# Narrow masked score pairs of the attention's row maxima share two PSUM banks

## The reference

```python
x = L0_attn_x                                   # (8, 1024, 256)
h = _layernorm(x) * (1 + ca) + sa
# attention, per head (16 heads, 48 channels for q and k, 16 for v)
scores = jnp.einsum('bhqd,bhkd->bhqk', q, k) * scale
scores = jnp.where(causal[None, None], scores, -jnp.inf)
attn = jax.nn.softmax(scores, axis=-1)
out = jnp.einsum('bhqk,bhkd->bhqd', attn, v)
x = x + ga * (out @ W_o)
h = _layernorm(x) * (1 + cb) + sb
# experts: t = (h @ Wm + bm) in parts of 32; softmax of logits over 16 experts, two are kept
hmid = gelu(einsum('td,edi->tei', t, W1) + b1); eo = einsum('tei,eio->teo', hmid, W2) + b2
x = x + gb * (comb @ Wo + bo)
```

## Time and profile before

| what | value |
|---|---|
| median of 3 runs | 2950.63 us (2949.89 to 2953.15) |
| span of the profiled execution | 2947.5 us; the page gives no other time for it |
| TensorE busy (modelled ends) | 2823.2 us, 96% |
| VectorE busy | 1869.7 us, 63% |
| ScalarE busy | 1806.7 us, 61% |
| GpSimd busy | 1243.5 us, 42% |
| score pairs of the maxima, L418 | 1536 matmuls |

### The profile page before, as it was taken

The page is one execution under the profiler, slowest core; times in us unless marked ns, Lnnn a source line. Parts: engine busy times, 40 slices in busy tenths (PEclk is TensorE's granted clock), DMA queues, the critical chain, the costliest instruction groups (busy, mean ns, idle before and its releaser), DMA issues.

```text
span 2947.5 us, 51530 instructions
## 1 busy us (share of the span) xinstructions
PE 2823.2 (96%) x16460; PEld 1254.0 (43%) x16460; DVE 1869.7 (63%) x4636; ACT 1806.7 (61%) x2148; POOL 1243.5 (42%) x1325
## 2 busy tenths in 40 slices
PE   6789999999999999999999999999999999999999
PEld 2344444444444444444434444444444444444433
DVE  5665766756667566666666666675756657666553
ACT  1346675566755667456674576655766566655687
POOL 4311555126551364413644146531465225661254
PEclk9889999999999999999999999999999999999999
DMA  6303443034430444204432044321553124531243
GB/s 141 73 1 84 113 121 96 4 98 112 133 73 2 106 123 118 70 8 119 121 100 70 21 128 122 90 56 29 134 130 91 34 63 115 130 84 27 74 129 93
DMA packets 177556, 253.06 MB, mean 86 GB/s; under 512 B 51085, under 2 KB 83869, under 8 KB 177197
## 3 DMA queue, kind: packets, MB, share of 16 engines
q1 hardware_dynamic: 170300, 247.79, 32.9%
q10 hardware_dynamic: 6996, 1.99, 0.3%
HBM read 159.13 MB, written 12.63 MB: 58 GB/s over the span
## 4 chain that ended last, share of the span: by engine, by line
PE 85%; DVE 6%; issue 3%; ACT 2%; POOL 1%; SPq 0%; DMA 0%; ACTq 0%; DVEq 0%; POOLq 0%
PE ps L1236 17%; PE ps L1272 17%; PE ps L1290 16%; PE ps L1256 9%; PE ps L418 8%; PE ps L464 4%; PE ps L505 2%; PE ps L466 2%; PE ps L535 2%; DVE front L561 1%; PE ps L516 1%; DVE rest L1392 1%; PE ps L492 1%; PE ps L523 1%; PE ps L450 1%
## 5 line engine op out<-in xcount | busy, mean ns | idle before, releaser
L1356 ACT ACTIVATE rest<-ps 128x1024 f32<-128x1024 f32 x1024 | 993.7, 1024 | 341.2 <-PE ps L1272 341.1
L1338 ACT ACTIVATE rest<-ps 128x1024 f32<-128x1024 f32 (+3 forms) x768 | 608.6, 810 | 550.1 <-PE ps L1236 536.4
L1456 POOL TENSOR_TENSOR rest<-rest 128x512 f32<-128x512 f32 x478 | 631.9, 1322 | 560.6 <-DVE rest L1392 550.1
L1392 DVE SCALAR_TENSOR_TENSOR rest<-ps,b2c,wide 128x512 f32<-128x512 f32 x512 | 383.8, 750 | 490.4 <-PE ps L1290 460.7
L1272 PE MATMUL ps<-wide,w1s 98*128 98x512 f32 x2048 | 644.6, 434 | 11.5 <-ACT rest L1356 8.7
L1290 PE MATMUL ps<-rest,w2s 128*32 128x512 f32 x4096 | 546.1, 605 | 0.6 <-ACT rest L1356 0.6
L1446 POOL TENSOR_SCALAR_AFFINE_SELECT rest<-rest 128x256 f32<-128x256 f32 x512 | 204.3, 407 | 806.7 <-ACT rest L1338 803.6
L558 DVE CUSTOM_DVE_ANT_0 rest<-ps,maskd 128x256 f32<-128x256 f32 (+3 forms) x1024 | 458.7, 487 | 121.9 <-PE ps L418 114.6
L1236 PE MATMUL ps<-wide 49*128 49x512 f32 (+3 forms) x2304 | 485.7, 511 | 7.2 <-ACT rest L1338 6.1
L1272 PEld LDWEIGHTS ps<-wide,w1s 98*128 98x128 f32 x2048 | 346.0, 189 | 238.4 <-ACT rest L1356 109.4
L561 DVE TENSOR_REDUCE front<-ps 128x1 f32<-128x512 f32 x512 | 329.1, 685 | 103.7 <-PE ps L418 99.9
(11 more groups left out here) (138 smaller groups left out, 2225.0 us busy)
## 6 DMA issues: line engine op xcount, KB each, us to landing
wide<-gate_rows SPq DMA_DIRECT2D x1024, 128.0 KB, 2.8
wide<-front SPq DMA_DIRECT2D x480, 64.0 KB, 2.0
wide<-front SPq DMA_DIRECT2D x192, 128.0 KB, 2.4
ao<-in_x SPq DMA_DIRECT2D x16, 512.0 KB, 5.0
heads<-front SPq DMA_DIRECT2D x64, 128.0 KB, 2.4
xs<-in_x SPq DMA_DIRECT2D x16, 512.0 KB, 5.1
out<-xs SPq DMA_DIRECT2D x32, 256.0 KB, 2.7
wide<-ao SPq DMA_DIRECT2D x96, 64.0 KB, 2.3
```

Source lines behind the costliest of these rows:

```text
L1338: nc.scalar.activation(L.pt[:, u % PTS, :, f:HALF], L.ps[:, 2 * (u % 2):2 * (u % 2) + 2, 0:HALF - f], ACT.Exp, scale=SCALE).then_inc(S["c_ ...
L1356: nc.scalar.activation(L.hm[:, u % HM, :], bank(2 * (u % 2), 2), ACT.Gelu).then_inc(S["e_gelu"], 1)
L1392: v.scalar_tensor_tensor(out=dst, in0=bank(L2 + q % 2), scalar=L.b2c[:, e:e + 1], in1=L.gb[:, q // 2 % GB, q % 2, :], op0=ALU.add, op1=ALU ...
L1456: g.tensor_tensor(dst, dst, L.gy[:, k % GY, :], ALU.add).then_inc(S["e_add"], 1)
```

## The change

The narrow masked pairs are joined two by two. Of the eight masked pairs of a half, the 128-key and the 384-key pair of the same `pr` share their two banks, and so do the two 256-key pairs; the two of 512 keys stay single. An item now carries a tuple of parts, `("pair", g, parts)`. TensorE waits for the two banks once, writes both parts into each bank side by side, four matmuls in direct sequence (first part upper and lower rows, second part upper and lower), and tells VectorE only at the last couple. VectorE reads first bank's parts, then the second bank's, with the same operations as before, and releases a bank after its last part; the wait for the scratch tile's last use stands at the first part alone.

A group has 18 issues for 24: `PAIRS[0]` is 5 items for 8, `PAIRS[1]` 13 for 16, in a new order in which the joined and the masked ones alternate with plain ones. `EARLY` is 3 for 4, so the opening computes a third item with 128 and 384 keys. The places are new: in images 1 to 7 slots 1, 2, 3, 5 and 7 have one item each, between; from slot 9 to 36 every slot has one between, and every even slot a second one behind: 47 items for 62. In the experts 25 of the slots 28 to 62 have an item, for 34.

```diff
--- before.py
+++ after.py
@@ -329,7 +329,18 @@
 
 
 SWAP = [(i + RD // 2) % RD for i in range(RD)]
-PAIRS = [[(i, n, pr) for i in range(4 * c, 4 * c + 4) for n in range(c + 1) for pr in range(2)] for c in range(2)]
+
+
+def masked_pairs(c):
+
+    i = 4 * c
+    shared = [(((i, c, pr), (i + 2, c, pr)),) for pr in range(2)] + [(((i + 1, c, 0), (i + 1, c, 1)),)]
+    return shared + [(((i + 3, c, pr),),) for pr in range(2)]
+
+
+PAIRS = [masked_pairs(0), [(((i, 0, pr),),) for i in range(4, 8) for pr in range(2)]]
+for k, pair in enumerate(masked_pairs(1)):
+    PAIRS[1].insert(2 + 2 * k, pair)
 ROWS = [(0, 0), (0, 1), (1, 0), (2, 0), (3, 0), (1, 1), (2, 1), (3, 1)]
 
 
@@ -369,7 +380,7 @@
                 done[e] += 1
                 self.frees.append((read[e], done[e]))
             self.end[item] = (read[e], done[e])
-            if item[0] == "pair" and item[3] == item[2] // 4:
+            if item[0] == "pair" and item[2][0][1] == item[2][0][0] // 4:
                 self.last_masked[item], masked = masked, item
 
     def last(self, bank):
@@ -408,15 +419,21 @@
     if kind in USES and not USES[kind]:
         return
     if kind == "pair":
-        g, i, n, pr = item[1:]
-        keys = key_range(i, n)
+        g, parts = item[1:]
         for name, count in R.moved[g]:
             pe.wait_ge(S[name], count)
         outs = [ring_write(pe, L, R, item, hh) for hh in range(2)]
-        for hh in range(2):
-            rows = slice(HP * hh, HP * hh + QD)
-            pe.matmul(outs[hh][:, 0:keys.stop - keys.start], L.q2[g][rows, pr, i * P:(i + 1) * P].bitcast(F32R),
-                      L.k2[g][rows, pr, keys].bitcast(F32R), start=True, stop=True).then_inc(S[R.filled], 1)
+        at = 0
+        for i, n, pr in parts:
+            keys = key_range(i, n)
+            w = keys.stop - keys.start
+            for hh in range(2):
+                rows = slice(HP * hh, HP * hh + QD)
+                mm = pe.matmul(outs[hh][:, at:at + w], L.q2[g][rows, pr, i * P:(i + 1) * P].bitcast(F32R),
+                               L.k2[g][rows, pr, keys].bitcast(F32R), start=True, stop=True)
+                if (i, n, pr) == parts[-1]:
+                    mm.then_inc(S[R.filled], 1)
+            at += w
         return
     if kind == "kc":
         R.wait(pe, L, ("std",))
@@ -544,21 +561,25 @@
         return
     read = S[R.read["v"]]
     if kind == "pair":
-        g, i, n, pr = item[1:]
-        w = key_range(i, n).stop - n * HALF
+        g, parts = item[1:]
         for hh in range(2):
             src = ring_read(v, L, R, item, hh)
-            m = (2 * hh + pr) * 4 + i % 4
-            dst = L.mx1[:, g, m, n:n + 1] if i // 4 else L.mx0[:, g, m:m + 1]
-            if n == i // 4:
-                past = R.last_masked[item]
-                if past:
-
-                    v.wait_ge(read, R.frees[R.start[past] + hh][1])
-                v.tensor_tensor_reduce(out=R.junk[hh][:, 0:w], in0=src[:, 0:w], in1=L.maskd[:, HALF - w:], scale=1.0,
-                                       scalar=-3e38, op0=ALU.add, op1=ALU.max, accum_out=dst).then_inc(read, 1)
-            else:
-                v.tensor_reduce(dst, src[:, 0:w], AX.X, ALU.max).then_inc(read, 1)
+            at = 0
+            for i, n, pr in parts:
+                w = key_range(i, n).stop - n * HALF
+                m = (2 * hh + pr) * 4 + i % 4
+                dst = L.mx1[:, g, m, n:n + 1] if i // 4 else L.mx0[:, g, m:m + 1]
+                if n == i // 4:
+                    past = R.last_masked[item]
+                    if past and at == 0:
+
+                        v.wait_ge(read, R.frees[R.start[past] + hh][1])
+                    ins = v.tensor_tensor_reduce(out=R.junk[hh][:, at:at + w], in0=src[:, at:at + w], in1=L.maskd[:, HALF - w:], scale=1.0,
+                                                 scalar=-3e38, op0=ALU.add, op1=ALU.max, accum_out=dst)
+                else:
+                    ins = v.tensor_reduce(dst, src[:, 0:w], AX.X, ALU.max)
+                at += w
+            ins.then_inc(read, 1)
     elif kind == "rmax":
         g = item[1]
         R.wait(v, L, ("pair", g, *PAIRS[1][-1]))
@@ -1062,12 +1083,9 @@
 
 
 AHEAD = 2
-EARLY = 4
-PLACES = [(0, 1), (1, 0), (2, 0), (3, 0), (4, 0), (4, 1), (5, 0), (7, 0), (8, 0), (8, 1)]
-PLACES += [(s, part) for s in range(9, 15) for part in range(2)] + [(15, 0), (15, 1)]
-PLACES += [(16, 0), (16, 1), (17, 0), (17, 1), (18, 0), (18, 1), (19, 0), (19, 1), (20, 0), (20, 1), (21, 0), (21, 1), (22, 0), (23, 0)]
-PLACES += [(s, part) for s in range(24, 30) for part in range(2)] + [(30, 0), (31, 0)]
-PLACES += [(s, part) for s in range(32, 37) for part in range(2)]
+EARLY = 3
+PLACES = [(1, 0), (2, 0), (3, 0), (5, 0), (7, 0)]
+PLACES += [(s, part) for s in range(9, 37) for part in range(2 - s % 2)]
 
 
 def attend_slots(img):
@@ -1077,14 +1095,14 @@
     if img:
         slots[1][1].extend([("out", 2), ("out", 3)])
         places = PLACES
-        pairs = [("pair", 1, *p) for p in PAIRS[1][AHEAD:AHEAD + 10]]
+        pairs = [("pair", 1, *p) for p in PAIRS[1][AHEAD:AHEAD + 5]]
         pairs += [("pair", g, *p) for g in (2, 3) for p in PAIRS[0]]
-        pairs += [("pair", 1, *p) for p in PAIRS[1][AHEAD + 10:]]
+        pairs += [("pair", 1, *p) for p in PAIRS[1][AHEAD + 5:]]
         pairs += [("pair", g, *p) for g in (2, 3) for p in PAIRS[1]]
     else:
-        places = [(k // 2, 0) for k in range(16 - EARLY)] + [(9 + k // 3, 0) for k in range(8)]
-        places += [(12 + k // 3, 0) for k in range(8)] + [(15 + k * 6 // 16, 0) for k in range(16)]
-        places += [(21 + k // 2, 0) for k in range(32)]
+        places = [(k * 6 // 10, 0) for k in range(13 - EARLY)] + [(9 + k // 2, 0) for k in range(5)]
+        places += [(12 + k // 2, 0) for k in range(5)] + [(15 + k * 6 // 13, 0) for k in range(13)]
+        places += [(21 + k * 16 // 26, 0) for k in range(26)]
         pairs = [("pair", 0, *p) for p in PAIRS[1][EARLY:]] + [("pair", g, *p) for g in (2, 3) for p in PAIRS[0]]
         pairs += [("pair", g, *p) for g in (1, 2, 3) for p in PAIRS[1]]
         slots[6][0].append(("rmax", 0))
@@ -1163,15 +1181,13 @@
     at(25, ("kc", 1), ("rope", 4))
     at(26, ("rope", 5))
     at(27, ("rope", 6), ("rope", 7))
-    for k, p in enumerate(PAIRS[0]):
-        at(28 + k, ("pair", 0, *p))
+    wanted = [(0, p) for p in PAIRS[0] + PAIRS[1]] + [(1, p) for p in PAIRS[0] + PAIRS[1][:AHEAD]]
+    steps = [28, 30, 32, 34, 35] + [37, 38, 39, 41, 42, 44, 45, 47, 48, 49, 50, 51, 52] + [53, 55, 57, 59, 60, 61, 62]
+    for q, (g, p) in zip(steps, wanted):
+        at(q, ("pair", g, *p))
     at(36, ("row", 0, 0))
-    for k, p in enumerate(PAIRS[1]):
-        at(37 + k, ("pair", 0, *p))
     at(53, ("rmax", 0))
     at(63, ("row", 0, 1), ("row", 1, 0))
-    for k, p in enumerate(PAIRS[0] + PAIRS[1][:AHEAD]):
-        at(53 + k, ("pair", 1, *p))
     return slots
```

## The result

| | before | after |
|---|---|---|
| median, on one chip | 2950.26 us (2947.39 to 2953.15, 4 runs) | 2931.45 us (2928.15 to 2934.93, 4 runs) |
| median, on a second chip | 2953.4 us (2943.77 to 2962.57, 12 runs) | 2928.49 us (2923.38 to 2941.02, 6 runs) |
| span of the profiled execution | 2947.5 us | 2932.8 us |

The ratio is 0.9934 (95% interval 0.992 to 0.9949) on the first chip and 0.9921 (0.9899 to 0.9944) on the second, where the changed kernel ran again beside two others. The forecast was 2932.

What follows compares the result with a forecast made beforehand. TensorE, busy 96% of the span, was taken as the bound. Images 1 to 7 at -2.1 us each (-14.8 in all), image 0 -4 and experts 0 gave -18.8 from 2950.6: 2932 us, range 2914 to 2950.

Steps and rivals of the forecast that it cites:

- slots 14, 22, 24 and 30: Images 1 to 7: two full issues cost 14, 22 and 30 +2.36 us; new bank waits in all four +1.0.
- second couples: The second part's matmuls in a joined issue cost 0.05 us each; twelve in slots 9 to 36 make +0.6.
- slots 0 to 8: Attention of images 1 to 7: fewer and moved pairs save 1.6 us an image.
- experts: Joined issue saves 0.14 us, slot after an emptied one pays 0.16: 0 an image, bounds -1.4 and +0.7.
- image 0 and opening: Image 0's slots 9 to 20: nine issues fewer at 0.45 us, -4 us, bounds 0 and -8; opening 0.
- Slot 0: Images 1 to 7: without its only pair, the rope takes the first bank and starts at once, -0.94 us.
- price of slot 18: Even slots 14, 22 and 30 become like slot 18, two full issues at 3.89 us: +2.36 us an image.
- chain of banks: In 14, 22, 24, 30 the first issue needs a bank of the odd slot's only issue: 0.25 us each, +1.0.
- Slots 4 and 8: Images 1 to 7: each loses two narrow pairs, one between the score couples and one behind, -0.98 us together.
- D: Rival, slower: second issue waits for both reads of the first in seven of fourteen even slots; 2968 us, chance 0.08.
- C: Rival, an even trade: bank chain costs 0.6 us, experts pay 0.1 to 0.3 more; 2946 us, chance 0.13.
- B: Rival: waits go, no new ones come, three narrow even slots stay near 3.4 us; 2908 us, chance 0.17.

Runs made afterwards that it cites:

- slot-0 run: Kernel before the change, with attention slot 0's pair moved out and early pairs of images 1 to 7 in slots 1 to 8: 2954.29 us, ratio 1.0007.
- unjoined run: Changed kernel, with each joined pair issued as two separate pairs of two banks each in the same place: 3151.06 us (one run).

## Why the prediction was right, and where its terms were off

The time came out at 2931.45 us for 2932, on a second chip at 24.9 us of gain for 18.8. The mechanism of images 1 to 7 was right, with their 15 us. That the gain on the first chip was the forecast one to a tenth of a us is luck: the traces give some 21.7 us (14.95 - 0.76 + 7.5 for image 0 at equal clock), and runs of the changed kernel differ by 7 to 18 us among themselves. Two balances came out by luck in part too. In the attention's -2.1 us slots 14, 22, 24 and 30 lost 0.55 us more than priced, 10 and 32 0.16, and those priced at nothing 0.25; the second couples, whose 0.6 are in these slots already, and slots 0 to 8 (0.3) made up for it. Image 0's attention came out at 180.15 us for 181 with its slots 0 to 3 5.4 us longer, by the clock, than before.

| term (us an image) | predicted | measured | |
|---|---|---|---|
| slots 0 to 8 | -1.6 | -1.90 | slot 0 -0.94, 8 -0.56, 4 -0.43, 5 -0.16, 1 +0.18 |
| slots 14, 22, 30 and 24 | +2.36 + 1.0 | +3.91 | +0.91, +1.10, +1.20, +0.69 |
| slots 10, 32 | +1.0 | +1.16 | |
| slots 15, 19 | -1.47 | -1.48 | 1.07 us each |
| slots 17, 21 | -2.5 | -2.55 | |
| slots 25, 27, 33 | -1.5 | -1.48 | 27 -0.61, as costed |
| second couples in slots 9 to 36 | +0.6 | in the slots | 0.05 for 128+384, 0 for 256+256 |
| the others | 0 | +0.25 | slot 20 +0.37, 34 +0.20, 35 -0.29 |
| attention in all | -2.1 | -2.09 | |
| experts | 0 | +0.09 | |
| image 0 and opening (us once) | -4 | -7.5 at equal clock, -9 to -11 in all | by the run that undid image 0's attention |

- **Slot 0** is right to 0.01 us: the rope waited for the third bank, not for VectorE as such. The slot-0 run shows the same 0.94 alone.
- **Even slots with two issues.** The price of slot 18 (3.89 us) was right for its kind (22 takes 3.93, 18 itself 3.89), and the chain of banks was real: 0.48 in slot 14, 0.34 in slot 30, 0.04 in slot 22. The mis-sized term is slot 24: costed 0.25, measured 0.69, of which 0.60 go when the five scalings on VectorE come later (and 0.62 when slot 22 has one issue). I had named them in the description of the kernel and had not put them into the chain, though a late read of slot 23 is what slot 24 waits for.
- **Slots 4 and 8** gave 0.99 us together for 0.98 costed. The 0.3 by which slots 0 to 8 came out better are slot 5 (-0.16, costed at nothing) and the second couples, which cost less there than the 0.14 counted.
- **Experts.** Both halves of the cancellation were as costed: the emptied slot's successor +0.17 us (0.16), the second couple 0.05 for 128+384 and 0 for 256+256 (0.05).
- **Image 0.** The mis-sized term is "-4, bounds 0 and -8". It priced slots 9 to 20 alone, at 0.45 us an issue, an estimate with no row of its own, and it held: 5 us at the same clock for 9 issues, 0.55 each. It left out slots 21 to 36 (-1.6) and slots 4 to 8 (-0.85), where issues go too, and it read the clock in image 2 only: in image 0's attention it is 0.93 before, and part of slots 9 to 20 ran at 1.2 GHz.
- **The rivals.** D's point was an even slot that loses over 0.19 us more than costed in all fourteen; three clearly did (24 by 0.44, 20 by 0.37, 14 by 0.23), and the fourteen together lost 5.5 us for 4.4 priced, under 0.1 each. C needed a bank chain of 0.6 in each of four slots and experts dearer by 0.1 to 0.3; the chain cost 0.39 on average, the experts 0.09. B's short even slots came only in the run that took their second issue away.

What stays open: no run keeps the joined issues at the old places, so joining and placing are told apart only slot by slot; and whether fewer handings over keep the clock up in image 0, as it fell behind five of nine stops in the experts of the unjoined run, or whether the difference of the means (0.89 against 0.83 over nine profiles) is chance.

## What to carry to other kernels

Count a merge of small matmuls not by what it saves on the engine but by the places it frees: here a joined issue itself brought 0.14 us (0.25 + 0.37 - 0.48), and each of the slots 15, 17, 19 and 21 that lost its second issue 0.6 to 1.35. Then count what the places that fill up take back: slots 9 to 36 together kept 0.18 us of it, and 1.90 of an image's 2.09 us came from slots 0 to 8, where five issues stand for ten. In a ring of few banks, price each issue by its reader: who reads the bank that it takes, and what else stands before that read in the reader's queue. And do the accounting for a first pass that is ordered differently by itself, with its own clock.

## What was unexpected of the hardware

- The granted clock of equal code falls differently in each execution: slots 9 to 20 of image 0 with the same order ran at 0.77 to 1.00 and took 51.14 to 42.16 us. A difference of 5 us in one profile of this kernel can be that alone.
- Two couples in direct sequence cost 0.05 us more than one when the first has 128 columns, and nothing when it has 256 or 384 (0.48, 0.435 and 0.43 us in all).
- A stop of TensorE of 1.13 us by the record, in work that ran at 2.4 GHz before and after, was followed by a lower clock (0.72 and 0.74 in the two slots behind), which cost as much again as the stop (1.4 us). Five of the nine such stops of an image's experts were followed by it; what set them apart from the other four is not shown.
